# Values by batch, another early order, and layer-norm statistics of tiles 6 to 9 on ScalarE in a gated cross-attention and FFN kernel

## What is computed

```python
x = x + tanh(g_xattn[0]) * xattn(layernorm(x), ctx)     # x: 2 x 1024 x 256, ctx: 2 x 77 x 256
x = x + tanh(g_ffn[0]) * ffn(layernorm(x))
# xattn: q = x @ Wq, k = ctx @ Wk, v = ctx @ Wv, 8 heads of 64, softmax(q k^T / 8) v, then @ Wo + bo
# ffn: inputs, weights (1024 x 256, 256 x 1024) and biases rounded to 8-bit fixed point;
#      relu(fixed(w1 x + b1)), then w2 h + b2
# layernorm: (x - mean) / sqrt(var + 1e-5), no gain or bias
```

## Time and profile before

| | |
|---|---|
| median of 3 runs | 124.15 us (124.11 to 124.31) |
| the profiled execution's own time | 123.75 us |
| its span, first to last instruction | 122.0 us |
| busy: PE, DVE, POOL, ACT | 115.0, 97.3, 87.3, 77.2 us |
| granted clock of TensorE | 1.000 over the span |

### The profile page before, as it was taken

The page is one execution under the profiler, slowest core; times in us unless marked ns, Lnnn a source line. Parts: engine busy times, 40 slices in busy tenths (PEclk is TensorE's granted clock), DMA queues, the critical chain, the costliest instruction groups (busy, mean ns, idle before and its releaser), DMA issues.

```text
span 122.0 us, 2891 instructions
## 1 busy us (share of the span) xinstructions
PE 115.0 (94%) x1013; PEld 104.9 (86%) x1013; DVE 97.3 (80%) x219; ACT 77.2 (63%) x168; POOL 87.3 (72%) x160
## 2 busy tenths in 40 slices
PE   7899995999999989999999999999999999999990
PEld 2589974999797989999999999999999997987880
DVE  2009789799999999899999999989797969437981
ACT  4168682968769895995757484848482919347420
POOL 3003757689498989899888949894989495996620
PEclk9999999999999999999999999999999999999999
DMA  2989799300000000000020002000200020020104
GB/s 73 340 236 370 254 371 377 145 0 5 3 0 3 8 0 0 0 0 5 0 86 5 0 0 86 0 3 5 86 0 0 3 91 0 0 86 8 65 21 172
DMA packets 5312, 8.87 MB, mean 73 GB/s; under 512 B 1175, under 2 KB 2226, under 8 KB 5170
## 3 DMA queue, kind: packets, MB, share of 16 engines
q1 hardware_dynamic: 5210, 8.61, 19.9%
q10 hardware_dynamic: 88, 0.08, 0.2%
HBM read 6.59 MB, written 2.10 MB: 71 GB/s over the span
## 4 chain that ended last, share of the span: by engine, by line
PE 61%; DVE 17%; ACT 8%; POOL 4%; issue 4%; DMA 3%; SPq 0%; ACTq 0%; DVEq 0%; POOLq 0%
PE of_ps L815 18%; PE sc_ps L782 13%; PE h_ps L842 9%; PE of_ps L857 7%; PE tr_ps L794 5%; DVE probs L573 3%; DMA wk_sb<-in_L_xattn_Wk_dram 3%; DVE mx L568 3%; DVE den L580 2%; ACT probs L403 2%; PE tr_ps L718 2%; ACT pT L430 2%; PE tr_ps L764 2%; DVE pT L609 1%; PE tr_ps L857 1%
## 5 line engine op out<-in xcount | busy, mean ns | idle before, releaser
L815 PE MATMUL of_ps<-u_sb,pT 128*128 128x256 f32 x240 | 31.1, 281 | 0.9 <-ACT x2T L450 0.8
L782 PE MATMUL sc_ps<-a_sb,xT 128*128 128x308 f32 x192 | 31.2, 311 | 0.7 <-DVE probs L573 0.7
L815 PEld LDWEIGHTS of_ps<-u_sb,pT 128*128 128x128 f32 x240 | 29.5, 188 | 1.9 <-issue 1.9
L403 ACT ACTIVATE probs<-probs,rstd 128x616 f32<-128x616 f32 x16 | 13.1, 816 | 26.1 <-DVE probs L573 25.8
L782 PEld LDWEIGHTS sc_ps<-a_sb,xT 128*128 128x128 f32 x192 | 27.5, 189 | 1.5 <-issue 1.3
L444 ACT ACTIVATE hid_q<-h_ps,b1z 128x256 int8<-128x256 f32 x58 | 24.7, 491 | 3.9 <-PE h_ps L842 3.9
L282 POOL TENSOR_TENSOR probs<-probs,rden 128x616 f32<-128x616 f32 x16 | 19.5, 1221 | 1.5 <-DVE rden L583 1.5
L331 POOL CAST hid<-hid_q 128x512 bf16<-128x512 int8 x27 | 15.8, 611 | 2.0 <-ACT hid_q L444 2.0
L842 PE MATMUL h_ps<-x2T,w1T 128*128 128x256 bf16 x128 | 16.6, 273 | 0.0
L568 DVE TENSOR_REDUCE mx<-sc_ps 128x8 f32<-128x616 f32 x16 | 12.6, 790 | 4.2 <-PE sc_ps L782 4.2
L842 PEld LDWEIGHTS h_ps<-x2T,w1T 128*128 128x128 bf16 x128 | 12.4, 98 | 1.6 <-ACT x2T L450 0.3
(11 more groups left out here) (113 smaller groups left out, 176.9 us busy)
## 6 DMA issues: line engine op xcount, KB each, us to landing
w_sb<-in_L_ffn_w_dram SPq DMA_DIRECT2D x2, 1024.0 KB, 11.1
out_dram<-x_sb SPq DMA_DIRECT2D x7, 256.0 KB, 2.5
x_sb<-in_x_dram SPq DMA_DIRECT2D x4, 256.0 KB, 8.1
x_sb<-in_x_dram SPq DMA_DIRECT2D x1, 1024.0 KB, 10.0
wk_sb<-in_L_xattn_Wk_dram SPq DMA_DIRECT2D x1, 512.0 KB, 4.0
wq_sb<-in_L_xattn_Wq_dram SPq DMA_DIRECT2D x1, 512.0 KB, 5.0
wv_sb<-in_L_xattn_Wv_dram SPq DMA_DIRECT2D x1, 512.0 KB, 7.8
wo_sb<-in_L_xattn_Wo_dram SPq DMA_DIRECT2D x1, 512.0 KB, 8.8
```

Source lines behind the costliest of these rows:

```text
L403: nc.scalar.activation(probs_v(T), probs_v(T), ACT.Exp, scale=rstd1[:, T:T + 1]).then_inc(exp_done, 1)
L782: ins = nc.tensor.matmul(sc_ps[:, a, 0:HALF], xT[:, T % 2, p, c, :], a_sb[:, q, T // TB, c, HALF * a:HALF * a + HALF], start=first, stop=last)
L815: ins = nc.tensor.matmul(attn_ps, pT[:, T % 2, p, P * c:P * c + P], u_sb[:, q, MC * (T // TB) + c, :], start=first, stop=last)
```

## The change

It has four parts.

1. **Values.** Before, the values of both batches were computed two heads' pairs at a time, 154 columns (2 x 77) a matmul. Now `valuesT(0)` and `valuesT(1)` compute batch 0 alone (77 columns a matmul), and `valuesT(2)` computes all four pairs of batch 1, behind `scores(1)` and before slot 0. It waits until DVE has freed its PSUM bank (`u_ready`). Its copy, `v_copy(2)`, stands on ACT before slot 0, ahead of exp(1).
2. **Early order.** The second copy of the keys goes from ACT to DVE. ACT copies xT of the first two tiles in two instructions. On ACT `xT_copy(2)` comes ahead of `exponentials(0)`. The low part of one group of output weights goes from DVE to POOL. DVE takes the statistics of tiles 4 and 5 behind center(1) and not ahead of the denominators of tile 0. POOL's `hidden_bias` and `output_bias` go from before the loop to slot 0, behind `softmax_scale(1)`; its `rstd_first` moves from odd slots (and the prologue) to even ones.
3. **Statistics.** For tiles 6 to 9 DVE has no `stats_first`. In slots 2 to 5 ACT has, per tile, a mean (Identity with scale 1/256 and an accumulator), then xn as before, waiting for that mean, then a variance (Square of xn with scale 1/16 and an accumulator).
4. **x2T earlier.** In slots 2 to 5 `rowsT_second(s-2)` stands right behind `xT_copy`, ahead of xn and the hidden units.

```diff
 # the main new and moved lines, by engine
+ON_ACT = 6, 7, 8, 9
...
+        v_banks = of_ps[:, 1, 0:MP], tr_ps[:, 0:MP], h_ps[:, 0, 0:HALF]
+        v_pairs = (0, 0, (0, 1)), (0, 2, (2, 3)), (1, 0, (0, 1, 2, 3))
...
             rstd_first(2, 4)
-            rstd_first(4, 6)
             softmax_scale(0)
             bias_rows()
-            hidden_bias()
-            output_bias()
+            u_low(0, 1)
...
                 if s == 0:
+                    hidden_bias()
+                    output_bias()
                     a1_parts(1)
-                if s % 2 == 1 and 3 <= s < TILES - 4:
-                    rstd_first(s + 3, s + 5)
+                if s % 2 == 0 and 2 <= s < TILES - 2:
+                    rstd_first(s + 2, s + 4)
...
             def minus_centred(T):
 
-                act.wait_ge(mv1_ready, T + 1)
+                if T in ON_ACT:
+                    act.wait_ge(x_in[min(T, TB) // 2], 16)
+                    if T > ON_ACT[0]:
+                        act.wait_ge(var_ready, T - ON_ACT[0])
+                    nc.scalar.activation(unused[:, :], x_sb[:, T, :], ACT.Identity, scale=1.0 / D,
+                                         accum_out=mv1[:, T, 0:1]).then_inc(mean_ready, 1)
+                    act.wait_ge(mean_ready, T - ON_ACT[0] + 1)
+                else:
+                    act.wait_ge(mv1_ready, by_dve(T) + 1)
                 act.wait_ge(xT_psum, T - 1)
                 nc.scalar.activation(xn[:, T % 2, :], x_sb[:, T, :], ACT.Identity, bias=mv1[:, T, 0:1],
                                      scale=-1.0).then_inc(xn_ready, 1)
+
+            def deviation(T):
+
+                act.wait_ge(xn_ready, T - 1)
+                nc.scalar.activation(unused[:, :], xn[:, T % 2, :], ACT.Square, scale=1.0 / 16,
+                                     accum_out=mv1[:, T, 1:2]).then_inc(var_ready, 1)
...
             minus_centred(3)
-            act.wait_ge(v_psum, 2)
-            nc.scalar.copy(values_of(1), values_psum(1)).then_inc(v23_ready, 1)
+            v_copy(1)
+            xT_copy(2)
             exponentials(0)
-            xT_copy(2)
             u_copy(0, 0)
             u_copy(0, 1)
+            u_copy_whole(0, 1)
             u_copy(0, 2)
-            minus_centred(4)
             act.wait_ge(g_in, 32)
             nc.scalar.activation(tg[:, :], g_sb[:, :], ACT.Tanh).then_inc(tg_ready, 1)
+            v_copy(2)
...
-                if live(s + 4) and s > 0:
+
+                if 2 <= s < 6:
+                    rowsT_second(s - 2)
+                if live(s + 4):
                     minus_centred(s + 4)
+                if s + 4 in ON_ACT:
+                    deviation(s + 4)
...
-                if s >= 2:
+                if s >= 6:
                     rowsT_second(s - 2)
...
             center(0)
-            stats_first(4, 6)
             rowsT_low(2)
             denominators(0)
             u_low(0, 0)
-            u_low(0, 1)
             center(1)
             u_low(0, 2)
+            stats_first(4, 6)
...
-                if 1 <= s and live(s + 5):
+                if 1 <= s and live(s + 5) and s + 5 not in ON_ACT:
                     stats_first(s + 5, s + 6)
...
+            def valuesT(n):
+                b, first, pairs = v_pairs[n]
+                for j in pairs:
+                    at = M * (j - first)
+                    for c in range(DK):
+                        ins = nc.tensor.matmul(v_banks[n][:, at:at + M], wv_sb[:, c, P * j:P * j + P],
+                                               ctxT[:, c, M * b:M * b + M], start=(c == 0), stop=(c == DK - 1))
+                ins.then_inc(v_psum, 1)
...
             scores(1)
+            pe.wait_ge(u_ready, 1)
+            valuesT(2)
```

More of the change, by code:

```diff
@@ L221, in flamingo_kernel, with by_dve @@
         block = stack.enter_context(nc.Block())
+        def by_dve(T):
+            return T - len([t for t in ON_ACT if t < T])
         def live(T):
@@ L272, in rstd_first @@
                 t = slice(first, end)
-                pool.wait_ge(mv1_ready, end)
+                if first in ON_ACT:
+                    pool.wait_ge(var_ready, end - ON_ACT[0])
+                else:
+                    pool.wait_ge(mv1_ready, by_dve(end))
                 if first == 0:
@@ L304, in a1_parts, with u_low @@
                                         ALU.subtract).then_inc(a1_low, 1)
[L306 to L310, removed]
+            def u_low(b, n):
+                pool.wait_ge(u_high, 3 * b + n + 1)
+                pool.wait_ge(u_copied, 1 if b == 0 else 2 + n)
+                nc.gpsimd.tensor_tensor(u_of(b, n, 1), u_whole[:, n, :], u_of(b, n, 0).bitcast(F32),
+                                        ALU.subtract).then_inc(u_low_pool, 1)
             def bias_rows():
@@ L418, in a1_copy, with u_copy_whole, v_copy @@
                 nc.scalar.copy(a_part(a1_whole[:, c, :], half), a_psum_of(c, half, 1)).then_inc(a1_copied, 1)
-            def u1_copy(n):
-                act.wait_ge(u_psum, 4 + n)
-                nc.scalar.copy(u1_whole[:, n, :], u_banks[1, n]).then_inc(u1_copied, 1)
+            def u_copy_whole(b, n):
+                act.wait_ge(u_psum, 3 * b + n + 1)
+                if (b, n) == (1, 1):
+                    act.wait_ge(u_low_pool, 1)
+                nc.scalar.copy(u_whole[:, n, :], u_banks[b, n]).then_inc(u_copied, 1)
+            def v_copy(n):
+                act.wait_ge(v_psum, n + 1)
+                if n == 0:
+                    act.wait_ge(vz_zero, 1)
+                nc.scalar.copy(values_of(n), values_psum(n)).then_inc(v_ready, 1)
             def u_copy(b, n):
@@ L475, in _ @@
             nc.scalar.copy(ctxT[:, :, :].rearrange("p c n -> p (c n)"), sc_ps[:, 0, 0:DK * MP]).then_inc(ctxT_ready, 1)
[L476 to L479, removed]
+            act.wait_ge(k_psum, 1)
+            nc.scalar.copy(kT[:, 0:2, :].rearrange("p c m -> p (c m)"), tr_ps[:, 0:2 * MP]).then_inc(k01_ready, 1)
             for j in range(2):
@@ L489, in _ @@
             a_copy(3)
-            act.wait_ge(xT_psum, 2)
-            nc.scalar.copy(xT[:, :, 0, :, :].rearrange("p i c n -> p i (c n)"),
-                           of_ps[:, 0, :].rearrange("p (i n) -> p i n", i=2)).then_inc(xT_high, 2)
+            for T in range(2):
+                act.wait_ge(xT_psum, 2)
+                nc.scalar.copy(xT[:, T, 0, :, :].rearrange("p c n -> p (c n)"), of_ps[:, 0, D * T:D * T + D]).then_inc(xT_high, 1)
             a1_copy(2)
             a1_copy(3)
-            act.wait_ge(vz_zero, 1)
-            act.wait_ge(v_psum, 1)
-            nc.scalar.copy(values_of(0), values_psum(0)).then_inc(v01_ready, 1)
+            v_copy(0)
             minus_centred(2)
             minus_centred(3)
-            act.wait_ge(v_psum, 2)
-            nc.scalar.copy(values_of(1), values_psum(1)).then_inc(v23_ready, 1)
+            v_copy(1)
+            xT_copy(2)
             exponentials(0)
-            xT_copy(2)
             u_copy(0, 0)
             u_copy(0, 1)
+            u_copy_whole(0, 1)
             u_copy(0, 2)
-            minus_centred(4)
             act.wait_ge(g_in, 32)
             nc.scalar.activation(tg[:, :], g_sb[:, :], ACT.Tanh).then_inc(tg_ready, 1)
+            v_copy(2)
             for s in range(TILES):
@@ L803, in attend @@
                 if T == 0:
[L804 removed]
+                    pe.wait_ge(u_ready, 2)
+                    pe.wait_ge(u_low_pool, 1)
                     pe.wait_ge(bo_rows, 1)
                 if T == TB:
[L807 to L808 removed]
+                    pe.wait_ge(u_ready, 3)
+                    pe.wait_ge(u_low_pool, 3)
                     pe.wait_ge(bo_rows, 2)
@@ L911, in _ @@
                 pe.wait_ge(wqT_ready, j + 1)
-                pe.wait_ge(k_ready, j + 1)
+                if j == 0:
+                    pe.wait_ge(k01_ready, 1)
+                else:
+                    pe.wait_ge(k23_ready, 1)
                 for c in range(DK):
```

48 lines of the change are left out of this document (25 added, 23 removed).

## The result

In 13 executions of each kernel on one chip, the kernel after took 124.67 us (median, 124.33 to 125.20), the kernel before 123.71 us (123.41 to 124.31): a ratio of 1.0067 with a 95% interval of 1.0050 to 1.0084. The change makes the kernel slower by 0.5 to 0.8%. The profiled span went from 122.0 to 122.9 us, +0.9, with +0.8 forecast.

What follows compares the result with a forecast made beforehand. PE, fully busy from 60 to 98 us, was taken as the bound, so attend(6)'s start decides: POOL 0.8 us late and ACT with four T of 1.55 give +0.8, span 122.8, median 124.9 us; range 123.4 to 125.8.

Steps and rivals of the forecast that it cites:

- The sum: Whole kernel: attend(6) on PE starts 0.8 us later, so the span is 122.8 and the median 124.9 us.
- POOL's late scale(2): POOL, slots 1 and 2: bias groups behind scale(1) make scale(2) 0.8 us later, and probsT(2) on PE with it.
- T: ACT, tiles 6 to 9: time from the mean to the next instruction, 1.55 us a tile, bounds 1.33 and 1.75.
- the rest of ACT's stretch: ACT from x2T(0) at 33.4 to exp(7) at 54.15: 14.55 us besides the four T of 1.55.
- No separate step is listed for the accumulator in the order: Argument for the rival of free accumulators on ACT (T = 1.33): no change, 124.25 us; chance of no change 0.17.
- 0.12 us a pass: PE's values groups of 77 columns: third group ends at 20.56, exp(1) at 21.05; first two give some 0.1 us each.
- It is worth only what PE can take up ... at most 1.2 us: DVE, four slots: statistics leaving it save 0.55 us a tile, 2.2 us, of which PE takes up at most 1.2.
- x2T earlier ... helps attend(3) and attend(4) ... but not attend(6): ACT, slots 2 to 5: attend(3) and attend(4) lose their long wait; mean, square and w2T's copy still precede exp(7).
- parts without cost: Includes POOL's inverse deviations: one slot earlier, still before the exp that needs them, tile 4's only just.
- With POOL not late at all PE's own work is the limit, -1.2: PE's limit at attend(6) against 56.69, in the rival of cheap values, faster, 123.75 us; chance of faster 0.25.

Runs made afterwards that it cites:

- e1: Kernel after with POOL's two bias groups moved back before the loop, behind the new part of u; ratio to the kernel before 0.9974.
- e7: Kernel after without accumulators on ACT's two activations, mean and variance of tiles 6 to 9 set to 0.5; ratio to the kernel before 1.0062.
- e11: e9 with the statistics of tiles 6 to 9 back on ACT; ratio to the kernel before 0.9971.
- e3: Kernel after with bias groups back before the loop and statistics of tiles 6 to 9 back on DVE; ratio to the kernel before 0.9930.
- e9: e3 with POOL's inverse deviations rstd_first(4, 6) moved from slot 2 to the end of slot 1; ratio to the kernel before 0.9881, 122.44 us.
- e8: Kernel before with only x2T moved ahead of xn and the hidden units on ACT in slots 2 to 5; ratio 0.9973.
- e12: e8 with POOL's pairs of inverse deviations one slot later, tiles 6 and 7 in slot 4; ratio to the kernel before 0.9943.
- e10: Kernel before with only POOL's two bias groups moved behind scale(1); ratio to the kernel before 1.0100.
- e2: Kernel after with the statistics of tiles 6 to 9 back on DVE, all else as changed; ratio to the kernel before 0.9991.
- e4: Kernel before plus statistics of tiles 6 to 9 on ACT and early x2T in slots 2 to 5; ratio to the kernel before 1.0047.

## Why the prediction was right

**The sum.** Forecast were 124.9 us, 0.75 over the 124.15 then known of the kernel before; measured were 124.67, 0.96 over 123.71. That the two totals lie 0.23 apart is in part luck, since the kernel before was timed 0.44 lower this time; the step is what the prediction is to be held to. Its path, from POOL's late scale(2) over x2T(0) and a full ACT to attend(6), is the one that the trace and e1 show. At attend(6) the errors partly cancel: +0.25 for POOL, -0.09 for T, +0.03 for the rest of ACT's stretch, -0.08 from exp(7) on, together 57.59 for 57.48.

**T.** Taken 1.55 us (the working gives 1.53) between bounds of 1.33 and 1.75, measured 1.53 on average of four tiles. The accumulator is written by an instruction of its own, as guessed; in tile 6 it starts 0.32 after its activation's start, overlaps it by 0.10, and a dependent xn starts 0.04 after its end. The own-engine wait of 0.03 to 0.04, borrowed from DVE, held on ACT too, and T without accumulators was 1.31 in e7 for the bound of 1.33. "No separate step is listed for the accumulator in the order" was no evidence.

**Values.** 0.12 us a pass taken, 0.114 measured: the third group starts at 18.64, the next matmul, rowsT(3), at 20.47, 1.83 us for 16 passes. exp(1) came at 20.98, with 21.05 forecast. Timeline of the kernel after, PE and ACT, which answers to the earlier trace rows:

```profile
18.64 1.99 PE L774 MATMUL h_ps<-ctxT,wv_sb 128*128 128x77 f32 x16
...
20.67 0.42 ACT L458 COPY vz<-h_ps 128x308 f32<-128x308 f32 x1 [1.75 <-PE h_ps L774]
20.98 0.82 ACT L431 ACTIVATE probs<-probs,rstd 128x616 f32<-128x616 f32 x1
```

The rule of the Trainium skill, "TensorE: Matmul & The Clock Gate", section LDWEIGHTS, gave 107 ns a pass; the trace, at 114, lies about half way between it and my 120. The first two groups go faster, 8 passes from 11.61 to 12.42 and from 14.21 to 15.05, 0.101 and 0.105 us a pass, so they give some 0.2 us each and not 0.1. Before, 8 passes of 154 columns took 1.05 us, 0.131 each: half the columns save a fifth, and far from half, as my 0.12 and the rule both said.

**POOL.** scale(2) +0.8 forecast, +1.05 measured. Scale(1) was earlier by 0.52 for 0.45; the stretch from there to scale(2) grew by 1.57 (6.95 for 5.38) and not by 1.27: the groups take 1.51 instead of 1.45, the first of them starts 0.13 later behind the scale than the copy of `a` did, and only 0.07 of the 0.18 of waiting was saved. The size was 0.25 too low, the mechanism right. x2T(0) at 33.65 for 33.4.

**ACT.** 20.7 us from x2T(0) to exp(7) for 20.75 (14.55 + 4 x 1.55), no idle time in it, exp(7) at 54.34 for 54.15, attend(6) at 57.59 for 57.5 and waiting for x2T. This part of the sum held as worked out, and e1 and e11 gave the same 20.7 with other starts.

**What was wrong or missing.** (1) "It is worth only what PE can take up ... at most 1.2 us" for DVE's relief: the most that a pair of traces shows is 0.53 us at attend(5) (e1 against e3), nothing where POOL no longer hangs on DVE (e11 and e9: 40.51 and 40.49), and in no run does any of it reach attend(6). Every kernel that gives DVE its statistics back is faster than its twin. (2) "x2T earlier ... helps attend(3) and attend(4) ... but not attend(6)" holds with ACT full; alone it gives 0.37 us (e8), and only POOL keeps it from more: there attend(4) comes 0.89 earlier, and then probsT(5) waits for scale(5). (3) The inverse deviations stood under parts without cost, and POOL was not named as a chain of its own through slots 2 to 5; their place is worth 0.65 us at attend(6) (e9) and 0.39 us at the end (e12). These errors didn't move the sum, since with the statistics on ACT that engine ended last. (4) "With POOL not late at all PE's own work is the limit, -1.2": e9 reaches -1.43 at attend(6).

## What to carry to other kernels

Idle time on an engine absorbs work only if it lies behind the instruction that came late; when a late value feeds the next step of every engine, the idle times travel with it, and much of the lateness arrives: 1.30 of 1.59 us in e10, 1.40 of 1.41 from e1 to the kernel after, 0.76 of 1.37 from e3 to e2. So price a moved group of small instructions by what stands behind it in its own queue, even on an engine that is busy only 72% of the time. And before giving an engine's work away, see which engine ends last once the work has moved: here ACT, with 0.6 to 1.6 us of idle time a slot, was filled up to relieve DVE, and then ACT was the one that attend(6) waited for. And before you read a difference of some tenths of a us between two traces, look where it first appears: in e4 0.36 us of it came from the first transfers of x.

## What the runs showed of the hardware that was not expected

- ACT's accumulator is a second instruction of some 0.19 us that overlaps its activation by 0.10, so it costs 0.09 to 0.10 us, where the smallest activation takes 0.21.
- PE can run the key matmuls at a slower rate in one execution and not in another. In the profiled execution of e1 they took 464 ns each, before 293, and the score weights so started at 10.96 for 8.75. In both, the record of the granted clock shows 1.00 there. Groups of one source line (count, min/median/max ns, first and last start), of the kernel before and then of e1:

```profile
L718 PE MATMUL tr_ps<-ctxT,wk_sb x16: 292/293/399, 5.3 to 7.3; 128*128 128x154 f32 x16
```

```profile
L756 PE MATMUL tr_ps<-ctxT,wk_sb x16: 462/464/627, 5.3 to 9.4; 128*128 128x154 f32 x16
```

The ratio of the two is 1.6. The profiled execution of e9 has the slower rate too (median 464 ns), with the score weights at 11.13. What decides it was not found.
